# Routing of a mixture of experts: each gate value by one multiplying and accumulating VectorE instruction of 192 numbers, in place of products and sums of 768

## What is computed

```python
h = h + attention(layernorm(h))                    # per sample: 561 tokens x 192
x = layernorm(h).reshape(-1, 192)
logits = x @ gate_w                                # gate_w: 192 x 8, one gate value per token and expert
probs = softmax(logits, axis=-1)
top_w, top_i = top_k(probs, 2)                     # two experts per token
combine = zeros((T, 8)).at[arange(T)[:, None], top_i].add(top_w)
y = einsum('tef,efd->ted', gelu(einsum('td,edf->tef', x, w_up) + b_up), w_down) + b_down
h = h + einsum('ted,te->td', y, combine)
```

## Time and profile before

| | |
|---|---|
| median of 3 runs | 4201.59 us (4197.65 to 4203.91) |
| the profiled execution | 4201.37 us, of which the span from first to last instruction is 4199.6 us |
| busy, share of the span | TensorE 3776.8 us (90%), VectorE 2410.2 (57%), ScalarE 2110.4 (50%), GpSimd 1134.8 (27%) |
| multiplications L1549, sums L1553 | 80 of each, 76.3 and 75.6 us of VectorE |
| granted TensorE clock | 0.947 of full speed on the mean |

### The profile page before, as it was taken

How to read it: one execution, slowest core, us unless ns; L and a number is a source line. 1 busy time by engine, 2 the same in 40 slices (tenths; PEclk the granted TensorE clock), 3 DMA queues, 4 the chain that set the end, 5 groups by cost and what they waited for, 6 DMA issues and landing times. The chain is left out here.

```text
span 4199.6 us, 64906 instructions
## 1 busy us (share of the span) xinstructions
PE 3776.8 (90%) x21662; PEld 2489.4 (59%) x21662; DVE 2410.2 (57%) x3929; ACT 2110.4 (50%) x3234; POOL 1134.8 (27%) x1036
## 2 busy tenths in 40 slices
PE   4899999999999999999984999999999999939998
PEld 3355555555555555555543676766666666628887
DVE  6566666666666666666642547566464655644443
ACT  0555545455554555545451666574665756613332
POOL 5132323223232333323222001111111121024444
PEclk7899999999999999999986999999999999969999
DMA  7242333423333233323335111111111111115564
GB/s 171 87 124 81 104 105 88 119 79 110 96 98 98 85 119 92 108 88 96 109 106 181 38 25 35 36 29 37 34 34 32 32 41 31 26 60 147 145 145 108
DMA packets 237689, 355.04 MB, mean 85 GB/s; under 512 B 40208, under 2 KB 138528, under 8 KB 234000
## 3 DMA queue, kind: packets, MB, share of 16 engines
q1 hardware_dynamic: 213344, 294.23, 24.3%
q0 software_dynamic: 23376, 57.40, 6.2%
q10 hardware_dynamic: 768, 0.79, 0.1%
HBM read 225.70 MB, written 112.63 MB: 81 GB/s over the span
## 5 line engine op out<-in xcount | busy, mean ns | idle before, releaser
L643 DVE TENSOR_REDUCE mx<-ring 128x2 f32<-128x1024 f32 x768 | 919.7, 1222 | 507.0 <-PE ring L406 503.3
L535 ACT ACTIVATE probs<-ring 128x1024 f32<-128x1024 f32 x768 | 767.2, 1024 | 416.6 <-PE ring L419 415.6
L1453 ACT ACTIVATE a_ring<-a_ring,a_nmx 128x561 f32<-128x561 f32 (+1 forms) x480 | 333.9, 696 | 239.5 <-DVE a_nmx L1737 238.0
L1737 DVE TENSOR_REDUCE a_nmx<-a_ring 128x1 f32<-128x561 f32 (+1 forms) x480 | 344.1, 735 | 191.5 <-PE a_ring L1392 96.2
L406 PE MATMUL ring<-k_stack,q_stack 48*128 48x512 f32 x1536 | 359.3, 480 | 63.9 <-ACT probs L535 23.3
L1292 POOL TENSOR_SCALAR_AFFINE_SELECT a_probs<-a_probs 128x256 f32<-128x256 f32 (+1 forms) x240 | 100.2, 418 | 1155.5 <-ACT a_probs L1489 1108.9
L419 PE MATMUL ring<-q_stack,k_stack 64*128 64x512 f32 x1536 | 362.9, 489 | 53.3 <-DVE mx L643 39.4
L433 PE MATMUL acc<-probs,vals 128*32 128x512 f32 x3072 | 399.7, 641 | 1.3 <-ACT probs L535 1.3
L1489 ACT ACTIVATE a_probs<-a_ring 128x561 f32<-128x561 f32 (+1 forms) x480 | 287.2, 636 | 179.0 <-PE a_ring L1392 175.9
L1392 PE MATMUL a_ring<-a_k_hh,a_q_hl 128*128 128x256 f32 (+1 forms) x960 | 312.4, 340 | 27.8 <-DVE a_q_hl L1717 12.7
L1392 PE MATMUL a_ring<-a_q_hl,a_k_hh 128*128 128x256 f32 (+1 forms) x960 | 289.7, 326 | 30.8 <-ACT a_ring L1453 21.5
(11 more groups left out here) (231 smaller groups left out, 6949.7 us busy)
## 6 DMA issues: line engine op xcount, KB each, us to landing
q_stack<-qk_scratch SPq DMA_DIRECT2D x576, 64.0 KB, 2.4
k_stack<-qk_scratch SPq DMA_DIRECT2D x576, 64.0 KB, 2.4
qk_scratch<-qk_hi SPq DMA_DIRECT2D x32, 768.0 KB, 3.6
qk_scratch<-qk_lo SPq DMA_DIRECT2D x32, 768.0 KB, 5.2
a_q_hm<-a_q_hl SPq DMA_DIRECT2D x48, 280.5 KB
a_k_hh<-a_k_hh SPq DMA_DIRECT2D x48, 280.5 KB
tokens<-h_out SPq DMA_DIRECT2D x33, 384.0 KB, 2.7
h_in<-tokens SPq DMA_DIRECT2D x32, 384.0 KB, 4.1
```

The costliest lines, as they stand in the source:

```text
L535: nc.scalar.activation(probs[n % 2][:, pair:pair + 2, x // 2, :], buf[:, :, :], ACT.Exp, scale=DK ** -0.5).then_inc(act, 1)
L643: nc.vector.tensor_reduce(mx[s][:, i, :].rearrange("p (r t) -> p r t", r=2)[:, :, t], buf[:, :, :], AX, ALU.max).then_inc(dve, 1)
L1453: nc.scalar.activation(buf, buf, ACT.Exp, bias=nmx[0:r, i, h:h + 1], accum_out=sums[0:r, i, h:h + 1]).then_inc(act, 1)
L1737: nc.vector.tensor_reduce(nmx[0:r, i, h:h + 1], flat(buf)[0:r, 0:N], AX, ALU.max, negate=True).then_inc(dve, 1)
```

## The change

The ten pairs ("mult", j), ("add", j) become 20 steps ("gate", i, h): tile i, experts 2h and 2h+1. A step is two instructions; each multiplies the tile's 192 numbers by one column of `gate`, writes the products to a quarter of `prod`, and accumulates their sum into one column of `logits` (`accum_out`). A step waits for the step two before it. The number of steps in the stream r stays the same, so every step of `A_ORDER` keeps its place.

```diff
-ROUTE = ([("r", x) for x in ("stats", "rsqrt", "norm")] + [("r", x, j) for j in range(10) for x in ("mult", "add")]
+ROUTE = ([("r", x) for x in ("stats", "rsqrt", "norm")] + [("r", "gate", i, h) for i, _ in TILES for h in range(4)]
...
-                elif what == "mult":
-                    j = step[2]
-                    after(*(("add", j - 1) if j else ("norm",)))
-                    row = xw[:, j // 2:j // 2 + 1, 0:D].to_broadcast([P, 4, D])
-                    ins = tt(prod[:, :, :], row, gate[:, 4 * (j % 2):4 * (j % 2) + 4, :], ALU.mult)
-                elif what == "add":
-                    j = step[2]
-                    after("mult", j)
-                    ins = add_up(logits[:, j // 2, 4 * (j % 2):4 * (j % 2) + 4], prod[:, :, :], AX, ALU.add)
+                elif what == "gate":
+                    i, h = step[2:]
+                    after(*(("gate",) + divmod(4 * i + h - 2, 4) if i or h >= 2 else ("norm",)))
+                    for e in (2 * h, 2 * h + 1):
+                        ins = stt(prod[:, e % 4, :], xw[:, i, 0:D], 1.0, gate[:, e, :], ALU.mult, ALU.mult,
+                                  accum_out=logits[:, i, e:e + 1])
                 elif what == "top":
-                    after("add", 9)
+                    after("gate", 4, 3)
```

## The result

The changed kernel takes 4162.37 us (median of 4 runs, 4160.74 to 4169.95), the kernel before 4199.62 in the same comparison: the ratio is 0.9915, with a 95% interval of 0.9902 to 0.9927. A second comparison gave 4166.49 (6 runs) against 4200.78 (17 runs), ratio 0.9919 (0.9906 to 0.9932). One execution on each side there was a slow one (4565.66 and 5958.43 us, at a granted clock of 0.78 and 0.55 of full speed); the ratio leaves both out. The direction was right; the size was off by a factor of 2.6.

The account below looks back on a forecast made before the run. It took attention's routing stretches as bound by VectorE and TensorE together, the last sample's gate values by VectorE alone. Gains of 3.8 us there and 10.5 inside attention, 14.3 together, gave 4187 us from 4201.37; range 4164 to 4208.

Parts of the forecast that it names:

- The bound and the two places: Attention stretches, seven times: VectorE 92%, TensorE 89% busy, a mixed bound; last sample's gate values: VectorE alone, every us counts.
- The price s of one accumulating instruction: VectorE's gate values: each of 40 instructions per sample on 192 numbers takes 0.40 us, between 0.26 and 0.56.
- The term for the last sample: Last sample's gate values, made alone: 16.0 us against 19.8, a gain of 3.8 us, all of it counting.
- the upper bound: Price of one accumulating instruction: VectorE's record of 0.357 us plus about 0.2 for the sum, s = 0.56.
- The lower bound: Price of one accumulating instruction if the sum came free: s = 0.26, from five independent instructions on 192 numbers.
- The wait: Gate steps: waiting for the step two before removes the old chain's 0.03 us per step, counted inside s.
- The term inside attention: Seven stretches: 16.0 us against 18.5 frees 2.5 of VectorE each, 0.6 of it counts, 1.5 each, 10.5 us in all.
- the free read: Accumulating instructions on VectorE: the sum's read costs nothing, so s = 0.26, the lower bound.
- the share of nine tenths: Strong end of the forecast's range: s = 0.34, 0.9 of VectorE's relief inside attention kept, 37 us gained, 4164.
- The separate read that doesn't overlap: Rival on VectorE: the accumulator's read follows its instruction without overlap, s = 0.45 to 0.50, kernel 4197 to 4208; chance 0.22.
- The doubled pass: Rival on VectorE: accumulating from two 4-byte SBUF tensors takes two steps per number, s = 0.60, kernel 4244; chance 0.13.
- The hidden case: Rival inside attention: TensorE sets the pace, only the last sample's 3.8 us count, kernel 4197.6; chance 0.08.

Follow-up runs that it names:

- the chained form: Changed kernel plus unused accumulating instructions on 192 numbers ahead of the last sample's top step, each waiting for the one ahead: 0.40 us each.
- The curve: Changed kernel with 8 of 192 numbers, one or two more accumulating instructions per step inside attention: stretches 33.3, 38.9, 42.7 us; changed 35.6, before 38.9.

## Why the prediction was wrong, point by point

**The bound and the two places: right.** Behind the first changed instruction, time came from the stretches inside attention (24.2 us in seven, the rest of the periods unchanged to 0.2) and from the last sample (8.5); each part done alone gave its share. One reading was loose: the stretch shown doesn't stand for all seven, since the seventh has less of VectorE's work and had a lower clock.

**The price s of one accumulating instruction: the step that failed.** "I take s = 0.40", the stream's 0.26 plus a complete record of a one-element instruction. It measured 0.28. The read has a record of its own (0.08 us, not 0.144 or 0.19), but it starts together with the next instruction and delays it by about 0.01 us. The term for the last sample was therefore 19.8 - 11.3 = 8.5 us in place of 3.8. ScalarE's rows, from which the upper bound came, don't carry over: there the instruction behind a read started 0.09 us after it. The lower bound's reading (0.26, read free) was the right one, and the sum's own 0.40 is what the chained form costs. The prediction took a record's length for the time that it takes from its engine, although its own rows of neighbouring instructions show records that overlap (1.39 us for five of 0.357).

**The wait: right in kind, too small in size.** It was put at 0.03 us per step, the gap behind the record of the instruction waited for. Start to start it adds 0.12 with the new form (and 0.11 with the old one, 0.99 against 0.88). The distant wait is worth 2.3 us on the last sample and next to nothing inside attention.

**The term inside attention: mis-sized, by the same price and partly set off by the share.** It forecast 2.5 us of VectorE per stretch and 0.6 of it counted, 10.5 us in seven. Measured from start to start, the new work is 40 x 0.28 = 11.2, so 18.5 - 11.2 = 7.3 us were freed, and 3.1 to 3.8 us per period were gained, 24.0 in all: a share of 0.47. By busy time (35.93 to 29.43) it is 3.3 of 6.5, 0.50. The curve shows why 0.6 was too high for so large a step: the share falls as VectorE gets idle. For a relief as small as the forecast 2.5 us it may have been about right, since the shares measured on either side of the old load are 0.54 and 0.63, but no run took off so little. Both errors together: 8.5 + 24.0 = 32.5 in place of 14.3. Had only s been right and the share been kept, the sum would have been 8.5 + 7.3 x 0.6 x 7 = 39 us, too much.

**The range.** Its low end (4164) came from s = 0.34 with nine tenths kept, so it never allowed for the free read, though that stood in the text as the lower bound. With the parts as measured the sum would be 4201.4 - 32.5 = 4168.9, which lies inside the range only by luck: the share of nine tenths, too high, made up for a price that was too high as well. The median of record lies below the range by 1.6 us, which the encoder's scatter between executions covers.

**The rivals.** The separate read that doesn't overlap (0.45 to 0.50) doesn't occur: even ahead of a wait the read starts 0.28 us after the start of an instruction whose record is 0.35 long (3694.51 and 3694.79), and the chained form costs 0.40. The doubled pass doesn't exist here: 768 accumulated numbers take 0.88 us, where it would be 1.6 or more. By the rule of the Trainium skill ("Vector Engine (DVE) Microarchitecture Reference", section "Points that are easy to get wrong") it had to be doubled; the trace disagrees, and the measurement decides. By the Trainium skill ("VectorE: DVE Perf Modes", section "Two Vector instructions with no wait between them") an instruction that also writes out its accumulator is two. The trace agrees, with 320 records of a read for 320 multiplications. The hidden case is refuted: the seven samples alone gave 26 us.

## What to carry to other kernels

Where products are summed along the free dimension on VectorE, one multiplying and accumulating instruction replaces two passes, and small pieces (192 numbers) don't eat up the gain; it is largest where nothing makes a piece wait for the one directly ahead (11.48 us against 13.79 here, and 19.99 for two passes). Price an unseen instruction from both ends, and if one end says that a part overlaps completely, let the range reach to it. And when an engine that is busy for 90% of a stretch is relieved, don't count the whole of it: here about half of the relief reached the kernel at first, and little of the next step. A kernel with the same work doubled and one with it nearly removed give that curve in two runs; read it from the whole period, not from the stretch alone.

## What the runs showed of the hardware that was not expected

- VectorE's read of the accumulator (record 0.08 us) starts in the same hundredth of a us as the next instruction, with 192, 384 and 768 numbers alike; behind ScalarE's (record 0.19 us) the next one starts 0.09 us after the read does.
- Writing the products as bf16 in place of 4-byte numbers changed nothing in the price: the last sample's gate values took 11.48 us in both forms.
- The encoder stage, with the same instructions, ended up to 12 us apart from one profiled execution to the next (first norm step 2535.0 to 2547.1 us over twelve), in step with the time that TensorE spent at its lower clock level (307 to 331 us), while the shown stretch inside attention repeated to 0.02 us over three profiles of the changed kernel. Kernels whose medians differ by less than that are better compared by their windows.
- A dip of 3.4 us to the lower level cost 1.8 us in a stretch where VectorE was busy 88 to 91% of the time, and nothing where it was busy 97%.
